# Scores contracted over all 128 rows and issued half a step ahead, expert weights turned within the first five items, first loads reordered over two queues

## The reference, cut to what matters

```
x: (32, 64, 256)   ctx_2048: (32, 64, 256)   mask: (32, 256, 256), added to the scores
# 1: item b is x[b] read as 64 channels by 256 positions; 8 heads of 8 channels
q, k = Wq @ LN(x) + bq, Wk @ ctx + bk;  v = Wv @ ctx + bv
x += tanh(g_xattn[0]) * softmax(q.T k / sqrt(8) + mask) v        # 32 items x 8 heads, 256 x 256 scores
# 2: 8 experts, token by token (2048 tokens of 256)
w = top_p(softmax(LN(x) @ router_w.T), 0.9)
x += tanh(g_ffn[0]) * sum_e w[:, e] * ((silu(h @ gate_w[e].T) * (h @ up_w[e].T)) @ down_w[e].T)   # h = LN(x), inner size 512
# 3: masked attention of LN(x) to ctx; 4: four experts over groups of 64 tokens
```

## Time and profile before

| | |
|---|---|
| Median of 3 runs | 1066.92 us (1066.81 to 1067.99) |
| Profiled execution | 1070.54 us, its span 1068.8 us |
| Busy share of the span | PE 81%, DVE 69%, ACT 54%, POOL 53% |
| DMA | 122.67 MB, mean 115 GB/s |

### The profile page before, as it was taken

How to read it: one execution, slowest core, us unless ns; L and a number is a source line. 1 busy time by engine, 2 the same in 40 slices (tenths; PEclk the granted TensorE clock), 3 DMA queues, 4 the chain that set the end, 5 groups by cost and what they waited for, 6 DMA issues and landing times.

```text
span 1068.8 us, 25000 instructions
## 1 busy us (share of the span) xinstructions
PE 869.6 (81%) x9015; PEld 686.4 (64%) x9015; DVE 742.1 (69%) x2490; ACT 576.8 (54%) x1258; POOL 565.3 (53%) x568
## 2 busy tenths in 40 slices
PE   2447677778999999999999999999999867866564
PEld 1224445556777777777777777777777756755464
DVE  1566777466877787787877778787777586565552
ACT  1357675445666676666666667666674213222222
POOL 4256454344777768676676867667664222221110
PEclk9855559799999999999999999999999989988877
DMA  4679996463767686677866777775764120000100
GB/s 137 168 148 237 212 218 158 110 122 67 143 126 146 120 141 132 132 147 133 138 122 132 138 125 146 133 138 118 130 106 71 59 91 11 20 23 21 32 20 21
DMA packets 319520, 122.67 MB, mean 115 GB/s; under 512 B 274716, under 2 KB 312612, under 8 KB 319396
## 3 DMA queue, kind: packets, MB, share of 16 engines
q1 hardware_dynamic: 319396, 121.07, 56.2%
HBM read 45.53 MB, written 8.39 MB: 50 GB/s over the span
## 4 chain that ended last, share of the span: by engine, by line
PE 49%; DVE 19%; ACT 9%; issue 8%; POOL 6%; DMA 5%; SPq 2%; POOLq 0%; DVEq 0%; ACTq 0%
PE psU L735 14%; PE psY L735 11%; PE psG L735 7%; PE ps L735 4%; PE psV L735 4%; DMA p_turn<-p_parts 4%; PE psT L735 3%; DVE ps L1081 3%; POOL hp_lo L520 2%; ACT p L618 2%; ACT p_parts L626 2%; PE psM L735 2%; POOL p_parts L528 2%; DVE th_ga_h L1176 2%; PE psV L895 2%
## 5 line engine op out<-in xcount | busy, mean ns | idle before, releaser
L528 POOL TENSOR_TENSOR p_parts<-p,p_parts 128x512 f16<-128x512 f32 x256 | 296.0, 1157 | 180.9 <-ACT p_parts L626 163.7
L520 POOL TENSOR_TENSOR hp_lo<-th_ga_h,hp_hi 128x512 f16<-128x512 f32 x128 | 149.0, 1164 | 171.0 <-ACT hp_hi L650 171.0
L735 PE MATMUL psU<-xT,w_gu 128*128 128x256 f16 x1536 | 195.6, 279 | 44.3 <-DVE th_ga_h L1176 32.3
L735 PE MATMUL psG<-xT,w_gu 128*128 128x256 f16 x1536 | 194.7, 278 | 14.6 <-issue 4.6
L735 PEld LDWEIGHTS psU<-xT,w_gu 128*128 128x128 f16 x1536 | 143.0, 99 | 87.9 <-DVE th_ga_h L1176 41.2
L735 PE MATMUL psY<-w_dn,hp_hi 128*128 128x256 f16 x1024 | 185.3, 276 | 11.1 <-POOL hp_lo L520 11.1
L735 PEld LDWEIGHTS psG<-xT,w_gu 128*128 128x128 f16 x1536 | 143.7, 99 | 54.7 <-issue 30.1
L618 ACT ACTIVATE p<-psT,exp_bias 128x256 f32<-128x256 f32 x256 | 107.2, 470 | 112.1 <-DVE exp_bias L1085 111.9
L626 ACT ACTIVATE p_parts<-p 128x512 f16<-128x512 f32 x256 | 161.6, 631 | 7.4 <-DMA p_turn<-p_parts 6.3
L1081 DVE CUSTOM_DVE_ANT_0 ps<-ps,mask_in 128x256 f32<-128x256 f32 x256 | 104.2, 448 | 84.4 <-PE ps L735 83.5
L618 ACT ACTIVATE p<-ps,exp_bias 128x256 f32<-128x256 f32 x256 | 107.2, 470 | 96.8 <-DVE exp_bias L1085 96.0
(11 more groups left out here) (154 smaller groups left out, 1109.1 us busy)
## 6 DMA issues: line engine op xcount, KB each, us to landing
mask_in<-in_mask_Bx2048x_ff SPq DMA_DIRECT2D x32, 256.0 KB, 3.1
part_scratch<-parts SPq DMA_DIRECT2D x16, 384.0 KB, 3.1
q_stack<-part_scratch SPq DMA_DIRECT2D x64, 96.0 KB
k_stack<-part_scratch SPq DMA_DIRECT2D x64, 96.0 KB
stage<-in_L_ffn_gate_w SPq DMA_DIRECT2D x8, 512.0 KB, 4.4
stage<-in_L_ffn_up_w SPq DMA_DIRECT2D x8, 512.0 KB, 4.4
stage<-in_L_ffn_down_w SPq DMA_DIRECT2D x8, 512.0 KB, 4.7
p_turn<-p_parts SPq DMA_TRANSPOSE x256, 3.4
```

Of the source, the lines that this page charges most:

```text
L520: pool.tensor_tensor(hp_lo[:, u % 2, :], hb32[:, u % 2, :], hp_hi[:, u % 2, :], ALU.subtract).then_inc(s["h_split"], 1)
L528: pool.tensor_tensor(p_parts[:, g % 4, 1, :, :], p32[:, g % 3, :, :], p_parts[:, g % 4, 0, :, :], ALU.subtract).then_inc(s["plo_done"], 1)
L735: return pe.matmul(out_, lhsT, rhs, start=start, stop=stop, skip_group_check=shares_bank)
```

## The change

1. `q_stack` gets a dimension for the head group: each group has its own tile of 128 rows, zero outside its 56 rows (two memsets on DVE, one for each parity; `k_stack` is set to one by POOL). The score matmuls read all 128 rows of both. The number of matmuls and their columns stay.
2. `scores(g+1)` is issued in half step g, after the unit and before `times_v(g-4)`.
3. `p32` has two buffers instead of three.
4. The 48 weight pieces: eight before step 0 (four ahead and four behind ACT's stack loads), then one in every half step of items 0 to 4. The loads are issued one every second half step. The units wait once for all pieces.
5. The start: Wq, Wk, x, ctx, Wv, mask and three weight loads in this order on SP; biases, router and gates on ACT's queue, each with a semaphore of its own. The first pair's qk is cut by DVE instead of POOL. The first pair's stacks are loaded half by SP, half by ACT. Statistics of later pairs of x start in step 0.

```diff
-        q_stack = eb("q_stack", [P, 2, 2, 4, D], BF16)
+        q_stack = eb("q_stack", [P, 2, 2, 2, 4, D], BF16)
...
-        p32 = eb("p32", [P, 3, 2, 256], F32)
+        p32 = eb("p32", [P, 2, 2, 256], F32)
...
+        def weight_at(g):
+
+
+            w = W_AHEAD + g
+            return (w // 6, w % 6 // 2, w % 2) if w < W_PIECES else None
...
+        def load_stacks(eng, par, q, piece):
+
+            eng.wait_ge(s["parts_stored"], 16 * (q + 1))
+            if q < 2:
+                eng.wait_ge(s["stacks_set"], 2)
+                eng.wait_ge(s["q_zeroed"], q + 1)
+            hh, i = piece // 2, piece % 2
+            lo = 64 * hh
+            src = [[part_d[par, w, c].rearrange("(g d r) n -> g d (r n)", g=2, d=DH)[hh]
+                    for c in range(3)] for w in range(2)]
+            eng.dma_start(
+                q_stack[lo + 24 * i:lo + 24 * i + 24, par, hh, :, :, :].rearrange("r b h n -> r (b h n)"),
+                src[0][i].unsqueeze(1).broadcast_to([DH, 3, 2048])
+            ).then_inc(s[f"stack{par}_loaded"], 16)
...
+            def load_weight_stage(c):
+
+                e, m = c // 3, c % 3
                 if e:
-                    sp.wait_ge(s["wgrp_T"], 6 * (e - 1) + 2 * (m + 1))
+                    sp.wait_ge(s["wgrp_T"], 2 * (c - 3) + 2)
...
-                    if n < NE and i in (2, 4, 6):
-                        load_weight_stage(n + 1, i // 2 - 1)
+                        load_stacks(sp, 1 - par, q + 1, i + 2)
+                    if i % 2 == 0 and 6 + g // 2 < 3 * NE:
+                        load_weight_stage(6 + g // 2)
...
+            load_small_weight(0, "wst_loaded")
+            load_small_weight(1, "wst_loaded")
+            sp.dma_start(x_res[:, 0:2, :], x_d[:, 0:2, :]).then_inc(s["x01_loaded"], 16)
+            sp.dma_start(ctx_in[:, 0, :], ctx_d[0]).then_inc(s["ctx0_loaded"], 16)
+            load_small_weight(2, "wv_loaded")
             load_mask(0, 0)
+            for c in range(3):
+                load_weight_stage(c)
+            sp.dma_start(ctx_in[:, 1, :], ctx_d[1]).then_inc(s["ctx1_loaded"], 16)
             load_mask(1, 1)
+            store_parts(0, 0)
+            for piece in range(2):
+                load_stacks(sp, 0, 0, piece)
             sp.dma_start(x_res[:, 2:16, :], x_d[:, 2:16, :]).then_inc(s["x_loaded"], 16)
-            store_parts(0, 0)
-            for piece in range(4):
-                load_stacks(0, 0, piece)
             store_parts(1, 1)
+            for c in range(3, 6):
+                load_weight_stage(c)
             sp.wait_ge(s["v_projected"], 1)
             sp.dma_start(ctx_in[:, 0, :], ctx_d[2]).then_inc(s["ctx0_loaded"], 16)
-            for m in range(3):
-                load_weight_stage(0, m)
 
             for n in steps:
...
 
+            pool.memset(k_stack[:, :, :, :, :], 1.0).then_inc(s["stacks_set"], 1)
             pool.memset(v_parts[:, :, :, :, :], 1.0).then_inc(s["stacks_set"], 1)
-            for piece in range(4):
...
-            act.wait_ge(s["small_loaded"], 16 * N_SMALL)
-            act.activation(gates[:, :], gate_in[:, :], ACT.Tanh).then_inc(s["gates_ready"], 1)
...
+            for w in range(2):
+                act.dma_start(bias_row[:, w, :], b_in[w].rearrange("(a n) -> a n", a=1)
+                              ).then_inc(s["brow_loaded"], 16)
+            act.dma_start(bias_v[:, :].rearrange("p (b n) -> p b n", b=2),
+                          A["L0_xattn_bv"].rearrange("(a b n) -> a b n", a=1, b=1).broadcast_to([P, 2, S])
+                          ).then_inc(s["bias_v_loaded"], 16)
+            act.dma_start(rt_in, A["L0_ffn_router_w"]).then_inc(s["rt_loaded"], 16)
+            for n, g in ((0, "g_xattn"), (2, "g_ffn")):
+                act.dma_start(gate_in[:, n:n + 2],
+                              A[g].rearrange("(a n) -> a n", a=1).broadcast_to([P, 2])
+                              ).then_inc(s["gate_loaded"], 16)
+            act.wait_ge(s["brow_loaded"], 32)
...
+                act.wait_ge(s["wst_T"], max(2, w + 1))
...
-                    src = psM[rows, w * S:w * S + S]
+                    src = psM[rows, w * S:w * S + S] if w < 2 else psY[rows, 1, 0:S]
...
-                if g >= 3:
-                    act.wait_ge(*low_done(g - 3))
+                if g >= 2:
+                    act.wait_ge(*low_done(g - 2))
...
+            act.wait_ge(s["gate_loaded"], 32)
+            act.activation(gates[:, :], gate_in[:, :], ACT.Tanh).then_inc(s["gates_ready"], 1)
+            for w in range(W_AHEAD // 2):
+                w_high(w // 6, w % 6 // 2, w % 2)
+            for piece in range(2, 4):
+                load_stacks(act, 0, 0, piece)
+            for w in range(W_AHEAD // 2, W_AHEAD):
+                w_high(w // 6, w % 6 // 2, w % 2)
...
-                    last = mm(score_bank(g)[:, nt, :], q_stack[64 * hh:64 * hh + 56, par, b2, hp, nt * P:nt * P + P],
-                              k_stack[64 * hh:64 * hh + 56, par, b2, hp, :])
+                    last = mm(score_bank(g)[:, nt, :], q_stack[:, par, hh, b2, hp, nt * P:nt * P + P],
+                              k_stack[:, par, b2, hp, :])
...
-                if tile == 0:
-                    pe.wait_ge(s["w_split"], 2 + copies)
-                    if ip == 0:
-                        pe.wait_ge(s["w_split"], 2 + 6 * (e + 1))
+                if u == 0:
+                    pe.wait_ge(s["w_split"], 2 + W_PIECES)
...
             project_qk(1, 1)
+            for w in range(W_AHEAD):
+                weight_transposes(w // 6, w % 6 // 2, w % 2)
+            pe.wait_ge(s["rt_loaded"], 16)
+            for k in range(KT):
...
-                    if g < 8 * B:
-                        scores(g)
-                    if n < NE and hp < 3:
-                        weight_transposes(n, hp, half)
-                        copies += 1
+                    w = weight_at(g)
+                    if w is not None:
+                        weight_transposes(*w)
                     u0, u2 = unit_at(n, hp, 0), unit_at(n, hp, 2)
                     if u0 is not None:
                         if half == 0:
-                            unit_gate(u0, copies)
+                            unit_gate(u0)
                         else:
-                            unit_up(u0, copies)
+                            unit_up(u0)
                     if u2 is not None:
                         unit_down(u2, half)
+                    if g + 1 < 8 * B:
+                        scores(g + 1)
                     if 4 <= g <= 8 * B + 3:
                         times_v(g - 4)
...
             for n in steps:
                 step(n)
...
+            dve.memset(q_stack[:, 0, :, :, :, :], 0.0).then_inc(s["q_zeroed"], 1)
...
-            dve.wait_ge(s["small_loaded"], 16 * N_SMALL)
+            dve.wait_ge(s["qk_copied"], 2)
+            st.link(dve.tensor_copy(parts[:, :, 0, :], qk32[:, :, :]))
+            st.link(dve.tensor_tensor(rem[:, :, :], qk32[:, :, :], parts[:, :, 0, :], ALU.subtract))
+            st.link(dve.tensor_copy(parts[:, :, 1, :], rem[:, :, :]))
+            dve.tensor_tensor(parts[:, :, 2, :], rem[:, :, :], parts[:, :, 1, :], ALU.subtract).then_inc(s["qk_split"], 1)
+            dve.wait_ge(s["bias_v_loaded"], 16)
             bias_to_v(0)
             norm1(1)
-            dve.wait_ge(s["x_loaded"], 16)
-            norm1_stats(2, 4)
+            dve.memset(q_stack[:, 1, :, :, :, :], 0.0).then_inc(s["q_zeroed"], 1)
+            for w in range(W_AHEAD):
+                w_low(w // 6, w % 6 // 2, w % 2)
...
+            dve.wait_ge(s["gates_ready"], 1)
...
-                    if n < NE and hp < 3:
-                        w_low(n, hp, half)
+                    w = weight_at(g)
+                    if w is not None:
+                        w_low(*w)
```

More of the change, by code:

```diff
@@ L625, in p_high @@
                     act.wait_ge(*turned(g - 4))
-                act.activation(p_parts[:, g % 4, 0, :, :], p32[:, g % 3, :, :], ACT.Copy).then_inc(s["phi_done"], 1)
+                act.activation(p_parts[:, g % 4, 0, :, :], p32[:, g % 2, :, :], ACT.Copy).then_inc(s["phi_done"], 1)
             def x_high(q):
@@ L738, in square @@
                 return psM[:, sl * P:sl * P + P]
[L743 removed]
             pe.wait_ge(s["consts_ready"], 3)
             for w in range(3):
[L746 removed]
+                if w != 1:
+                    pe.wait_ge(*((s["wst_loaded"], 32) if w == 0 else (s["wv_loaded"], 16)))
+                pe.transpose(psM[:, w * S:w * S + S] if w < 2 else psY[:, 1, 0:S], stage_w[0:S, w, :], ident[0:S, 0:S]).then_inc(s["wst_T"], 1)
             pe.wait_ge(s["bias_turned"], 2)
@@ L749, in _ @@
                 pe.transpose(psV[:, w:w + 1], bias_turn[:, w, :], ident[0:1, 0:1]).then_inc(s["biasT_ready"], 1)
-            for k in range(KT):
-                last = pe.transpose(psY[:, 0, k * NE:k * NE + NE], rt_in[:, k * P:k * P + P], ident[0:NE, 0:NE])
-            last.then_inc(s["router_T"], 1)
             def weight_transposes(e, m, k):
@@ L1028, in step @@
```

(1 more changed line is left out.)

91 lines of the change are left out of this document (29 added, 62 removed).

## The result

The kernel after takes 1021.57 us (median of 4 runs, 1017.67 to 1023.67) against 1066.87: a ratio of 0.9579, with a 95% interval of 0.9539 to 0.9619. Run once more later (e13), it took 1018.50 us, a ratio of 0.9531 (0.9503 to 0.9559). The forecast was 1012 us in a range of 982 to 1038, and the sign and the range held. The sum behind it was right for partly wrong reasons.

What follows compares the result with a forecast made beforehand. TensorE was taken to bound items 8 to 30, transfers items 0 to 4, a chain of waits items 5 to 7. Terms -0.6 + 8 - 41 - 21.6 = -55.2 us gave 1012 us, range 982 to 1038.

Steps and rivals of the forecast that it cites:

- The start: Up to the first scores: 33 us instead of 33.6, range 28 to 38, with loads reordered and qk split on VectorE.
- the second load of stage 0: At the start, weight pieces 6 and 7 wait for this load, queued behind the 1.8 MB of x: near 30.5 us.
- The second q memset: At the start, VectorE's second zeroing of q delays w_low(0); the estimate by the skill was 4.3 us.
- Items 5 to 7: Without weight pieces these become steady items but for the clock: 70 us for 111.0, -41 us, between -45 and -31.
- the clock falls back after item 5: Sign of being wrong: PE's granted clock should reach 1.00 for good within 10 us of the first unit.
- Items 0 to 4: Carrying 40 weight pieces instead of 30, transfers set the pace: 122 us instead of 114.0, +8, bounds 112 and 140.
- Items 8 to 30: Steady items: 0.9 us saved an item, bounds 0.2 and 1.5; 21.6 us for 24 items.
- the chain of half steps 5 to 7: Steady items, maxima to hp's low half: ends at most 0.4 us sooner in odd items, 0.1 in even ones.
- PE gets all of it: Rival, chance 0.16: VectorE keeps pace since scores come early, 1.45 us an item; -77, 990 us.
- in every odd item by more than 1 us: Sign of being wrong: PE waiting this often and this long for p_turn, the transposes of the probabilities.
- Rows and order: Score matmuls: 128 rows save 0.19 us a half step; scores half a step ahead start VectorE's maxima some 0.4 us sooner.
- p32 with two buffers: Makes exps(g) wait for p_low(g-2): costed at nothing, at most 1 us a pair of items if the cover goes.

Runs made afterwards that it cites:

- e13: The kernel after run once more, unedited, on the chip of e12: 1018.50 us, ratio 0.9531 to the kernel before.
- e2: Kernel after with GpSimd's fills of k_stack and v_parts put before its wait for the layer norm sums: 1013.76 us, ratio 0.9505.
- e1: Kernel after with the x load issued ahead of SyncE's store of the parts: 1013.75 us, ratio 0.9498.
- e11: Kernel after with six weight pieces instead of eight turned ahead of step 0: 1014.74 us, ratio 0.9498.
- e6: Kernel after with weights turned as before, six pieces in each of items 0 to 7, none ahead: 1027.98 us, ratio 0.9624.
- e12: Kernel after with both the weights by item of e6 and the spread stack pieces of e5: 1021.08 us, ratio 0.9547.
- e4: Kernel after with scores back at the head of their own half step, still on 128 rows: 1041.74 us, ratio 0.9755.
- e3: Kernel after with score matmuls reading 56 rows again instead of 128: 1029.33 us, ratio 0.9642.
- e5: Kernel after with SyncE's four stack pieces spread to half steps 5, 7 of even and 1, 3 of odd items: 1000.22 us, ratio 0.9368.
- e9: Kernel after with score matmuls reading 64 rows instead of 128: 1030.92 us, ratio 0.9653.

## Why the prediction was right, and where it was not

*The start, -0.6 forecast, +11.7 measured: the mis-sized term.* The forecast put the second load of stage 0 "near 30.5", behind the x load. The order was right and the time was 12.6 us off: its user started at 43.12. The forecast had the store landed near 16.5, and SyncE goes on to its stack loads, x and the second load only then. In the kernel after they begin at 23.91, 7.4 us later. 4.4 of that is xn beside the memsets (e2: 19.50); the other 3.0 are there without them: the first projection starts at 11.37 in e2 and not near 8. From there to the use of the load the forecast allowed 14.0 us and it took 19.2. Measured: 6.1 us for the x load (e1), 4.6 for xn beside the memsets (e2), 6.1 for the two pieces that need the second load (e11); these overlap. With the weights as before and all else as in the kernel after, the start is 33.2 (e6), with xn still at 4.74 us. So what the new order of loads won (the first projection starts at 11.37 in e2, at 14.00 in the kernel before) the held xn lost again, and the pieces ahead of step 0 cost 12 us. The second q memset, which the forecast put at up to 4.3 us, took 1.76. The split of qk moved to VectorE cost what was forecast, 18.79 to 21.13, 2.3 us.

*Items 5 to 7, -41 forecast, -43.9 measured.* Right. The weights alone are 34.6 (e6) to 36.5 us (e12); of the other 9, undoing the order gives back 4.7 (e4) and undoing the rows 0.9 (e3), the rest is open; the sum counted 0.9 an item there. The granted clock rose to 1.00 at 172.4 us, 3.7 us after the first gate group started at 168.67. It was not for good: it fell once in the steady part, from 315.8 to 319.2 us, behind the wait of 2.32 us at 314.54. That is the forecast's sign "the clock falls back after item 5". The fall follows the longest p_turn wait; in e5, which has no such wait, and in e13, whose longest is 1.9 us, the steady part stays at 1.00.

*Items 0 to 4, +8 forecast, +3.7 measured.* Right in sign. DMA share 0.92. e5 shows that this stretch too has 3.9 us of the bunched queue in it: 113.8 when spread.

*Items 8 to 30, -20.7 forecast, -22.9 measured: the right sum of two wrong halves.* The forecast said that the other engines take back 1.2 us a pair of items of what PE saves, because the chain of half steps 5 to 7 can't close up, and that transposes cost 0.2 a pair. Neither was so. With the transposes out of the way (e5) the stretch falls by 35.5 us, 1.54 an item: the rival "PE gets all of it" at 1.45, while the product wait stays (18.8 us, from 16.1). That is still not all that two edits could give: the rows save 0.21 in each half step, 1.7 an item, and the earlier scores came on top of them. And the transposes took 12.6 us, 1.1 a pair. The forecast had named p_turn waits "in every odd item by more than 1 us" as what would prove it wrong. They came in 9 of the 11 odd items and passed 1 us in 5 (in e13 in all 11, and 8). So the size of this stretch came out right by luck: what the forecast took off too much for the other engines, the transposes took instead.

*Rows and order.* The forecast gave 0.19 us a half step to the rows and used the earlier scores only to argue how much of it comes through. Undone one at a time, the order is worth more: from 533.6 us, 128 rows without the earlier scores give 6.5 (e4), the earlier scores without the 128 rows 15.1 (e3), both 22.9. These three carry the bunched queue, with 2.3, 6.1 and 14.5 us of p_turn waits, so the kernel with both edits pays most for it; neither edit was undone with the pieces spread, and how the 35.5 us divide there is open. That the rows gain at all stands on the ratios, 0.9642 and 0.9653 (e3, e9) against 0.9579 and 0.9531. The saving of the rows is real on PE (0.21), and how much of it passes on depends on when VectorE starts its maxima.

*p32 with two buffers.* ACT waited for p_low once in the steady part, 1.2 us in all, and no wait of PE names it. A kernel with three buffers was not tried.

## What to carry to other kernels

A queue that issues in program order makes a wait into a barrier: list for each queue what stands behind every wait, and put large transfers that need nothing ahead of the first of them. When the bound engine gets faster, check next the issuing queue of the transfers it consumes, by issue time per step, and keep bunches of issues apart there. Work that is moved ahead "for nothing" is paid at the start if even its last piece needs a second load, so undo each part alone before crediting it: here the part that carried the forecast was worth 21 of its 41 us in all, and spreading four pieces of a queue about as much (18 to 21).

## What the hardware showed that was not expected

- A VectorE tensor_scalar of 128x256 f32 took 4.67 and 4.87 us beside GpSimd memsets (after, e1) and 0.40 without them (e2), and ended just after the second memset (15.69 against 15.54). So the memsets held it, both of them in a row (10.66 to 14.17 and 14.11 to 15.54). The Trainium skill, SBUF — State Buffer, "Who interferes with whom", says that tensor_scalar can enter a mode in which VectorE contends with GpSimd for a shared pair of ports, and that whoever is first has it for the whole instruction. The trace agrees that the later one is held, with 4.67 us against 0.40. That xn stayed held over a second memset, queued behind the first, goes beyond that sentence.
- A change in the number of rows, 128 to 64 or 56 and back, costs PE 0.1 us at each side of a pair of matmuls of 256 columns, and 64 rows cost no less than 56. The weight load at the change starts with its matmul and not 0.11 us ahead of it (e3). The Trainium skill, TensorE: Matmul & The Clock Gate, "LDWEIGHTS (loading the stationary operand)", says that a weight load takes the same time whatever the rows. The trace agrees for the loads themselves, 94 ns with 56 rows (e3) and 98 with 128 (after); the gap of 0.32 against 0.22 us comes on top.
- One wait of 2.32 us on PE was followed by a gate group of 2.71 us, the length that the earlier trace rows shows at 1.2 GHz, against 1.48 in the earlier trace rows. The clock fell after the wait, as the window says, so the p_turn wait cost that item more than its own length:

```profile
315.70 2.71 PE L754 MATMUL psG<-xT,w_gu 128*128 128x256 f16 x12
```

```profile
315.80:319.20 3.40, 3.40 (x18) 2.35 (x17) 1.39 (x4) 0.88 (x3) 0.68 (x1) 0.51 0.73 137
```

- Issuing a 512 KB load took SyncE 5.45 us right behind the 1.8 MB of x and a store (29.80), 5.44 in e2 in the same place, and 0.54 where x had gone out 20 us before (e1, 29.54).
